# GNN, mixing and expert layers on one core: W1 is applied ahead of the aggregation from the second graph layer on, with dense chunks of 510 columns

## The reference, cut to what matters

```python
h = xn
for layer in range(6):
    agg = segment_sum(h[src], dst, num_segments=n)
    z = h + agg
    z = z @ W1[layer] + b1[layer]
    z = relu(batchnorm(z, g1[layer], be1[layer]))      # statistics over the 6250 nodes
    z = z @ W2[layer] + b2[layer]
    z = batchnorm(z, g2[layer], be2[layer])
    h = z if layer == 5 else relu(z)
x = x + h + mix(xn)          # per head: layer norms k, v; q @ (k.T @ v) / N, + xn
x = x + ffn(layernorm(x))    # 8 experts of three products each, weighted by a softmax router
```

## Time and profile before

| | |
|---|---|
| time, median of 3 runs | 3836.84 us |
| profiled execution, its own time | 3838.87 us |
| its span, first to last instruction | 3835.1 us |
| mean granted TensorE clock | 0.998 |
| TensorE matmul busy | 3670.9 us (96%), 26532 matmuls |
| VectorE, ScalarE, GpSimd busy | 2107.3, 1434.4, 2729.8 us |
| dense aggregation, L1090 | 9408 matmuls |
| slots, L1124 | 7128 matmuls, 1782 gathers |
| first product, L1146 | 936 matmuls |
| share of the chain that ended last | TensorE 81%, L1090 alone 47% |

### The profile page before, as it was taken

The page is one execution under the profiler, slowest core; times in us unless marked ns, Lnnn a source line. Parts: engine busy times, 40 slices in busy tenths (PEclk is TensorE's granted clock), DMA queues, the critical chain, the costliest instruction groups (busy, mean ns, idle before and its releaser), DMA issues.

```text
span 3835.1 us, 69586 instructions
## 1 busy us (share of the span) xinstructions
PE 3670.9 (96%) x26532; PEld 2042.9 (53%) x26532; DVE 2107.3 (55%) x6797; ACT 1434.4 (37%) x2684; POOL 2729.8 (71%) x2840
## 2 busy tenths in 40 slices
PE   2899999999999999999999999999999999999998
PEld 1455555555555555554545445555445556666666
DVE  9888866455473322544326343263222776777776
ACT  6666655011151111411005000050001777777776
POOL 5666664767766667667775777757775799999997
PEclk9999999999999999999999999999999999999999
DMA  6434352545426666365553656535553100000000
GB/s 219 144 121 154 124 184 89 189 161 182 165 95 202 207 217 193 103 216 198 171 168 118 213 178 211 177 118 172 167 170 105 70 22 12 23 12 23 12 14 10
DMA packets 206492, 511.08 MB, mean 133 GB/s; under 512 B 34849, under 2 KB 138766, under 8 KB 199632
## 3 DMA queue, kind: packets, MB, share of 16 engines
q0 software_dynamic: 86288, 235.82, 20.7%
q1 hardware_dynamic: 119872, 270.73, 19.6%
HBM read 417.44 MB, written 88.98 MB: 132 GB/s over the span
## 4 chain that ended last, share of the span: by engine, by line
PE 81%; DVE 7%; ACT 4%; DMA 4%; POOL 2%; issue 2%; SPq 0%; ACTq 0%; DVEq 0%
PE bank L1090 47%; PE bank L2187 5%; PE bank L2170 5%; PE bank L2155 5%; PE bank L1897 4%; PE bank L1124 4%; PE bank L1146 4%; DMA sg<-pieces_d,ssrc 3%; PE bank L895 2%; ACT h L2226 2%; ACT f L2227 1%; PE bank L1200 1%; POOL sg L1370 1%; DVE ohk L694 1%; DVE ohl L693 1%
## 5 line engine op out<-in xcount | busy, mean ns | idle before, releaser
L1090 PE MATMUL bank<-slab,pieces 128*128 128x500 fp8e4 (+1 forms) x9408 | 2321.2, 374 | 2.7 <-DVE slab L713 2.7
L1370 POOL DMA_INDIRECT sg<-pieces_d,ssrc x1782 | 1699.0, 953 | 760.6 <-PE bank L1124 348.7
L1090 PEld LDWEIGHTS bank<-slab,pieces 128*128 128x128 f16 (+1 forms) x9408 | 801.9, 97 | 631.2 <-issue 5.3
L1739 DVE TENSOR_SCALAR so<-iota,skey 128x32 f16<-128x32 f16 (+32 forms) x1782 | 407.5, 259 | 543.6 <-PE bank L1124 541.6
L1124 PEld LDWEIGHTS bank<-so,sg 128*128 128x128 f16 x7128 | 434.0, 96 | 397.1 <-DMA sg<-pieces_d,ssrc 35.2
L1301 ACT ACTIVATE zin<-bank 128x500 f16<-128x500 f32 (+2 forms) x156 | 85.6, 570 | 1127.0 <-PE bank L1090 803.2
L1124 PE MATMUL bank<-so,sg 128*128 128x32 f16 (+32 forms) x7128 | 464.1, 182 | 24.8 <-DMA sg<-pieces_d,ssrc 23.7
L2445 POOL TENSOR_SCALAR btmp<-bob,rw 128x256 f32<-128x256 f32 (+1 forms) x343 | 394.6, 1150 | 33.5
L2226 ACT ACTIVATE h<-bank,fscale 128x512 f16<-128x512 f32 (+2 forms) x416 | 314.7, 757 | 190.8 <-PE bank L2170 190.4
L842 ACT ACTIVATE slab<-bank 128x490 fp8e4<-128x490 f32 x400 | 272.2, 688 | 137.2 <-PE bank L895 134.4
L1314 ACT ACTIVATE z<-bank,prm,ct 128x500 f32<-128x500 f32 (+2 forms) x156 | 116.6, 751 | 543.4 <-DVE st L1744 543.3
(11 more groups left out here) (343 smaller groups left out, 3614.3 us busy)
## 6 DMA issues: line engine op xcount, KB each, us to landing
slab<-slabs SPq DMA_DIRECT2D x40, 3062.5 KB
pieces_d<-pieces SPq DMA_DIRECT2D x60, 512.0 KB
sg<-pieces_d,ssrc POOLq DMA_INDIRECT x1782
slabs<-slab SPq DMA_DIRECT2D x8, 3062.5 KB, 11.2
mx<-xnorm SPq DMA_DIRECT2D x24, 512.0 KB
ws<-L_ffn_W_dram SPq DMA_DIRECT2D x32, 256.0 KB, 4.3
experts<-wp SPq DMA_DIRECT2D x24, 256.0 KB, 2.7
mb<-mixed SPq DMA_DIRECT2D x11, 512.0 KB, 3.8
```

The source lines that it names most:

```text
L1090: ins = pe.matmul(psD[half][:, 0:w], PC[:k, a, c:c + P], v[:k, a, :], start=(r == 0), stop=(r == 97))
L1370: pool.indirect_dma_start(out=SG[j % RINGS][:, :], out_offset=None, in_=d_H[:, :], in_offset=bass.IndirectOffsetOnAxis(ap=SI[:, j:j + 1], ...
L1739: dve.tensor_scalar(SO[j % RINGS][:, 0:w], iota[:, 0:w], SK[:, j:j + 1], None, ALU.is_equal).then_inc(s_soh, 1)
```

## The change

From layer 1 on the product with W1 is done ahead of the aggregation. The h phase becomes a y phase: Z is scaled in groups of 512 columns (`YG`) by GpSimd into a ring of seven f32 buffers, ScalarE writes the Relu's high piece and VectorE the low piece over Z's place, and for each pair of tiles TensorE runs 12 matmuls of 256 columns (the h pieces are the stationary operand, W1's pieces the moving one). The result, multiplied by 2^-23, is split into `pieces` by ScalarE (now a Copy) and VectorE. The transposes, the scaling in place, and from layer 1 on zin and the product behind the aggregation are gone; VectorE takes statistics straight from the aggregation's banks and ScalarE writes Z from them (`dve_agg`, `act_agg`), and a bank is free when Z is written. Layer 0 works as before. The pairs sit 0.7 dense steps apart (the last at step 14), the first gather stands at step 35 and the slots run from step 75 to 1546.

Dense chunks are 510 columns wide, the sparse ones 414 and four of 439; there are 287 slots a layer and 816 windows in layer 0. Slabs are 2% larger. The mixture's groups are 3 tiles, 4 ten times, 3 and 3. One of the bias rows moves to another place in memory and is loaded after the last norm.

```diff
-WIDTHS = [500] * 8 + [430] + [455] * 4
+WIDTHS = [510] * 8 + [414] + [439] * 4
...
+YG = [(0, 256)] + [(256 + 512 * i, 512) for i in range(11)] + [(5888, 362)]
+YRING = 7
...
         for j in range(NPAIR):
-            add(1.5 * max(0, j - 4), "h", j)
-        g0, g1 = 100, STEPS * NDC - 26
+            add(0.7 * max(0, j - 4), "y", j)
+        g0, g1 = 75, STEPS * NDC - 22
...
             add(g, "slot_out", t)
+            if l:
+                continue
...
+            if l and t > 0 and s == 2:
+                out.append(("agg", t - 1, 1))
+            if l and s == 100:
+                out.append(("agg", t, 0))
...
+TILES_OF = [3] + [4] * 10 + [3, 3]
...
-                if r == 0 and t:
-                    pe.wait_ge(s_zlo[0], 2 * (NDC * l + t - 1) + half + 1)
+                if r == 0 and t and l:
+                    pe.wait_ge(s_gev, gemm_count(l, 0, t - 1, half))
+                elif r == 0 and t:
+                    pe.wait_ge(s_zlo[0], 2 * (t - 1) + half + 1)
...
-                    if i > NDC:
-                        pe.wait_ge(s_zlo[1], 2 * (NSC * l + i - 1 - NDC) + half + 1)
+                    if i > NDC and l:
+                        pe.wait_ge(s_gev, gemm_count(l, 0, i - 1, half))
...
                 if i >= 4:
                     pe.wait_ge(s_hlo, NPAIR * (l - 1) + i - 3)
...
-                for u in range(2 if i < NPAIR - 1 else 1):
-                    a = 2 * i + u
-                    k = rows(a)
-                    for m in range(2):
-                        ins = pe.transpose(psH[i % 4][:k, 256 * u + P * m:256 * u + P * m + P],
-                                           Z[:, m, a * P:a * P + k], ident)
-                ins.then_inc(s_htr, 1)
+                for j, (k, px, pw) in enumerate(PASSES):
+                    if i in YFIRST and pw == 0:
+                        pe.wait_ge(s_ylo if px else s_yhi, 2 * len(YG) * (l - 1) + 2 * g + k + 1)
+                    v = y_pieces(g, k)[px]
+                    for u, a in enumerate(tiles):
+                        ins = pe.matmul(psH[i % 4][:rows(a), D * u:D * u + D], v[:, a * P - c:a * P - c + rows(a)],
+                                        W1P[l % 2][:, k, pw, :], start=(j == 0 and u == 0), stop=(j == 5),
+                                        skip_group_check=True)
+                ins.then_inc(s_ymm, 1)
...
+    def y_ahead(j):
+
+        if j not in YFIRST:
+            return ()
+        g = YFIRST[j]
+        return (0, 1, 2) if g == 0 else (g + 2,) if g + 2 < len(YG) else ()
...
+    def act_y_high(l, g):
+        c, w = YG[g]
+        for m in range(2):
+            hi = y_pieces(g, m)[0]
...
+                act.wait_ge(s_yf, y_scaled(l, g, m))
+                act.activation(hi, RY[(2 * g + m) % YRING][:, 0:w], ACT.Relu).then_inc(s_yhi, 1)
+
+    def dve_y_low(l, g):
...
+            dve.wait_ge(s_yhi, 2 * len(YG) * (l - 1) + 2 * g + m + 1)
+            dve.scalar_tensor_tensor(out=lo, in0=RY[(2 * g + m) % YRING][:, 0:w], scalar=0.0, in1=hi, op0=ALU.max,
+                                     op1=ALU.subtract).then_inc(s_ylo, 1)
...
+    def pool_y(l):
         pool.wait_ge(s_bn, 2 * l)
+        for g, (c, w) in enumerate(YG):
+            pool.wait_ge(s_gev, y_done(l, g))
+            for m in range(2) if g else (1,):
+                n = 2 * g + m
+                if n >= YRING:
+                    pool.wait_ge(s_ylo, 2 * len(YG) * (l - 1) + n - YRING + 1)
+                pool.tensor_scalar(RY[n % YRING][:, 0:w], Z[:, m, c:c + w], scaled[:, m, 0:1], scaled[:, m, 1:2],
+                                   ALU.mult, ALU.add).then_inc(s_yf, 1)
...
+    def dve_agg(l, t, m):
+        if t < NDC:
+            dve.wait_ge(s_dense, 2 * (NDC * l + t) + m + 1)
+        else:
+            dve.wait_ge(s_smm, NSLOT * l + LAST_SLOT[t] + 1)
+        dve.bn_stats(st[0][:, m, stat_place(l, t), :], agg_bank(l, t, m)[:, 0:width(t)]).then_inc(s_stat, 1)
+
+    def act_agg(l, t, m):
...
+        act.wait_ge(s_stat, gemm_count(l, 0, t, m))
+        act.activation(Z[:, m, FIRST_NODE[t]:FIRST_NODE[t] + width(t)], agg_bank(l, t, m)[:, 0:width(t)], ACT.Identity,
+                       scale=ctl[l % 2][:, 0, 0:1], bias=prmcol("b1", l, m)).then_inc(s_gev, 1)
...
                 act.activation(PC[:k, 2 * i:2 * i + n, 0:D],
                                psH[i % 4][:k, 0:256 * n].rearrange("p (u f) -> p u f", u=n),
-                               ACT.Relu).then_inc(s_hhi, 1)
+                               ACT.Copy, scale=YS).then_inc(s_hhi, 1)
...
-            elif kind == "h":
-                for g in h_ahead(i):
-                    dve_h_affine(l, g)
+            elif kind == "y":
+                for g in y_ahead(i):
+                    dve_y_low(l, g)
```

More of the change, by code:

```diff
@@ L224, in layer_order @@
                     half_open = q == 2
[L225 removed]
+            if l == 0 and s == 100:
                 out.append(("zin", t, 0))
@@ L253 @@
 NG = 13
-FIRST = 3
+TILES_OF = [3] + [4] * 10 + [3, 3]
+FIRST = TILES_OF[0]
+assert sum(TILES_OF) == NT and len(TILES_OF) == NG
 def group(c):
-    if c == 0:
-        return list(range(FIRST))
-    return [a for a in range(4 * c - 4 + FIRST, 4 * c + FIRST) if a < NT]
+    return list(range(sum(TILES_OF[:c]), sum(TILES_OF[:c + 1])))
 def cols(c):
```

270 lines of the change are left out of this document (166 added, 104 removed).

## The result

The changed kernel takes **3828.92 us** (median of 20 runs, 3823.07 to 3834.57) against 3837.01 us for the kernel before (20 runs beside them): ratio 0.9976, 95% interval 0.9969 to 0.9982, 8.1 us less. Forecast were 23.3 us less, 3813.5. The profiled execution took 3826.26 us, its span 3822.4.

What follows compares the result with a forecast made beforehand. TensorE's instructions were taken as the bound, GpSimd's gathers close behind. Layers 1 and 2 -7.5, layer 1's waits -10.8, layers 3 to 5 -6, layer 0 +7.5, mixture's end -6.5: -23.3, so 3813.5 us; range 3788 to 3845.

Steps and rivals of the forecast that it cites:

- gathers late: Rival, layers 1 to 5: slow scaled tiles put the first gather at 49 us; 3856 us; 0.16 together with dearer matmuls.
- The rule weighed: Start of layers: if each GpSimd scaled tile waited for one VectorE low piece by the port lock, it would cost 1.53 us.
- The product a wash: Layers 1 to 5: product behind the aggregation gone, -32.0 us; product ahead of it, +32.0 us.
- dense matmuls +4.2 ns each: Layers 1 to 5: 1568 dense matmuls, ten columns wider, cost +6.5 us a layer.
- the rival of dearer matmuls: Dense matmuls of 510 columns cost more than their columns; 5 ns more each gives +47 us; 0.16 together with late gathers.
- Layer 1: TensorE's waits for wm and z and the lower clock behind them vanish, -10.8 us; 435 us told as sign.
- I keep nearly all of the present excess, 9 of 10.6: Layers 3 to 5: excess over the bound, read as slab loads delaying gathers, stays at 9 us: 423 each, -2 each.
- 14 more windows at 0.105: Layer 0: the added windows cost TensorE +1.5 us, part of +7.5.
- 5.9 us per expert should cover them: Mixture's last two groups: TensorE's 5.9 us per expert covers ScalarE and VectorE, saving 6.5 of 8.5 idle us.
- 49 and 44 us: Sign of a right forecast: the lengths of the last two groups of the mixture.
- waits of layer 1 stay: Rival: VectorE's mixture steps block banks or sparse cover instead, the 10.8 us come back; about 3829 us; chance 0.17.
- gathers stop binding: Rival: regular spacing removes the excess, layers 3 to 5 fall to 414 to 415; 3787 us; chance 0.17.

Runs made afterwards that it cites:

- undisturbed layers: Layers 3 to 5 with slab loads of 1 tile in place of 49 from layer 1 on: 3808.86 us for the kernel before, 3794.90 for the changed kernel.

## Why the prediction was wrong

- **Start of a layer, gathers late: right.** Scaled tiles 1.13 to 1.19 us (1.24 told), the sixth pair at 9.8 us (9.3 told), first gather 42.9 (42.8). The rival *gathers late* needed 1.46 us and falls.
- **The rule weighed: the rule agrees, the reading of it didn't.** The Trainium skill, "SBUF — State Buffer", Who interferes with whom, has a VectorE instruction with two SBUF inputs contend with a GpSimd one that reads SBUF. Of the 220 scaled tiles of 512 columns in the two profiles of the changed kernel, the 19 that overlap no such low piece, or one for under 0.05 us, take 0.76 us each; the 141 that overlap one for over 0.4 us take 1.39 on the mean, up to 1.80. So the trace agrees. What didn't hold was that every tile waits for a whole low piece (1.53 us): the mean is 1.16.
- **The product a wash, dense matmuls +4.2 ns each: right.** Twenty of 510 columns stand 0.2158 us apart, and the rival of dearer matmuls falls; layer 2 came out at 445.4 (444.7 told).
- **Layer 1: right.** 434.1 for 434.5; no wait took the place of those that vanished.
- **Layers 3 to 5, -0.6 for -6: the bounds right, the excess mis-sized.** Told were 415.6 by TensorE before and 414.0 by the gathers after, 1.6 less; undisturbed layers showed 415.9 and 414.4, 1.5 less. The step that failed is "I keep nearly all of the present excess, 9 of 10.6". Over the gathers' bound the excess was 10.0 on the mean before and is 9.8 now, so all of it stayed. The term also took layer 3's 424.9 for all three layers, which had 424.3 on the mean. Of the 5.4 us that are missing, 2.1 are this base, 2.3 the excess and 1.0 the bound. Measured against undisturbed layers, the excess grew from 8.4 to 9.8 a layer, so a gain of 1.5 and a loss of 1.4 left 0.2. The traces show where it grew: as many gathers are late as before (90 over 8 us in each first profile), TensorE's waits for them beyond those of undisturbed layers went from 19.8 to 21.7 us in the three layers, and what the lower clock costs from 2.6 to 7.7 us (means of two profiles; half of the time spent at that level). Together that is 29.4 us now, all of the 29.3, and 22.4 of the 25.2 before. The forecast didn't charge this clock here, though the earlier trace rows had shown it. Why the changed kernel waits longer at a time in layers 3 and 4 (3.4 and 3.6 us at most for 1.9 and 2.1, but 2.4 for 3.4 in layer 5) is argued, not shown: before, the gathers' bound (414.3) lay a little under TensorE's, so delayed gathers could catch up; now they alone are the bound.
- **Layer 0: +9.4 for +7.5.** The term "14 more windows at 0.105" priced TensorE's instructions and missed their place: the last of 102 windows moved towards the seam, and TensorE's waits there went from 2.7 to 6.7 us, 4.0 that stood in no term. The rest of the sum was then 2 us too high. With the distance set right layer 0 fell by 9, to 611.4, below the 613.2 of the kernel before, so the other terms of +7.5 aren't confirmed either.
- **The mixture's end: -2 for -6.5.** The step that failed is "5.9 us per expert should cover them", with the saving of 6.5 of 8.5 idle us. 5.9 is true for the experts alone; the first of the two groups carries the preparation of the next group, and the last one's chain at its end is as long as before, so TensorE's idle time fell by 0.5 us only. The prediction's own sign for these groups, 49 and 44 us, was 4.7 us under what its saving gives (104.2 - 6.5 = 97.7); measured are 54.3 and 52.5.
- **Small slips of the sum.** 24.5 pairs at 0.43 are 10.5, not 10.6; 1568 matmuls at 4.2 ns are 6.6, not 6.5; ten slots at 0.10 are 1.0, not 1.1. Together they make the gain of each of the five layers 0.3 us too large.
- **The total, and luck.** These three stages make 11.8 of the 15.2 us. The other 3.3 are the choice of the profiled executions; by the medians of the two series the change is worth 8.1 and 9.8 us. The range began at 3788 and ended at 3845, so it held the time. 8.1 us are a third of what was forecast, just past the 7.7 that the prediction calls no change. The rival *waits of layer 1 stay* named about 3829, and 3828.92 was measured; that is luck, since its waits were gone and layer 1 gained all that was told. The rival *gathers stop binding* didn't come true either, though without long slab loads layers 3 to 5 stand at its 414 to 415.

## What to carry to other kernels

When a saving on the busiest engine brings a stage down to another engine's bound, forecast the undisturbed stage and its excess apart, and don't let the excess shrink without a reason; charge each long wait of TensorE with the clock behind it. A large transfer beside small latency-bound gathers is worth splitting and spreading; here four parts some 7 us apart, the only split that was tried, were worth 33 us, four times the change itself. And when a tile becomes wider, redo every distance in the hand-written order that counts on the number of its pieces.

## What had not been expected of the hardware

A slab load of 3.1 MB made gathers that otherwise land 2.8 us after their issue take up to 11.3 us, and 9.5 us behind its own issue TensorE ran dry (1790.56 to 1800.03) for 2.9 us. With four loads of 0.8 MB, layer 3's slowest gather took 7.3 us and no wait for one was over 0.9. A wait of TensorE of 2.9 us was followed by at least 2.3 us at a granted clock of 0.50. And whole series came in which TensorE paused some 400 times for no cause that the trace shows, at 9 to 10% of the time.
